# The last block of a two-stage attention and expert kernel: keys turned a tile sooner, high parts first, two operations moved

## The reference, cut to what matters

```python
qp = _phi(proj(Wq, bq)); kp = _phi(proj(Wk, bk)); v = proj(Wv, bv)   # _phi(x) = elu(x) + 1
def step(carry, inp):
    kv, ksum = carry
    kt, vt, qt = inp
    kv = kv + jnp.einsum('bhd,bhe->bhde', kt, vt)
    ksum = ksum + kt
    num = jnp.einsum('bhd,bhde->bhe', qt, kv)
    den = jnp.einsum('bhd,bhd->bh', qt, ksum)[..., None] + EPS
    return ((kv, ksum), num / den)
...
x = x + _L0_attn_ref(_layernorm(x), ...)
probs = softmax(layernorm(x) @ gate_w.T); top2_w, top2_idx = top_k(probs, 2)
counts = jnp.bincount(top2_idx.reshape(-1), length=E); keep = counts <= cap
```

## Time and profile before

| | |
|---|---|
| median of 3 runs | 1963.82 us (1962.81 to 1964.63) |
| the profiled execution | 1965.99 us |
| its span, first to last instruction | 1964.2 us |
| TensorE matmul busy | 1913.2 us (97%) |
| VectorE busy | 1588.5 us (81%) |
| ScalarE busy | 663.9 us (34%) |
| GpSimd busy | 901.9 us (46%) |
| start of block 31 on TensorE | 1921.97 us |
| last instruction of VectorE | 1961.43 us |

### The profile page before, as it was taken

The page is one execution under the profiler, slowest core; times in us unless marked ns, Lnnn a source line. Parts: engine busy times, 40 slices in busy tenths (PEclk is TensorE's granted clock), DMA queues, the critical chain, the costliest instruction groups (busy, mean ns, idle before and its releaser), DMA issues. The chain is left out here.

```text
span 1964.2 us, 60624 instructions
## 1 busy us (share of the span) xinstructions
PE 1913.2 (97%) x25420; PEld 1678.0 (85%) x25420; DVE 1588.5 (81%) x3375; ACT 663.9 (34%) x1291; POOL 901.9 (46%) x982
## 2 busy tenths in 40 slices
PE   6899999999999999999999999999999999999996
PEld 5688888888888888888888888888888888888886
DVE  5687788887788987788887988787878898878786
ACT  2333333333333333332333333333333333333331
POOL 3445345545345545345545354544345544355422
PEclk8999999999999999999999999999999999999998
DMA  5223433323333333433323333233333233343222
GB/s 182 87 82 109 130 114 120 116 80 125 125 109 125 99 102 114 124 121 114 109 90 123 120 119 120 92 110 114 125 125 109 89 107 126 113 129 121 72 73 75
DMA packets 168032, 218.02 MB, mean 111 GB/s; under 512 B 24272, under 2 KB 81616, under 8 KB 167760
## 3 DMA queue, kind: packets, MB, share of 16 engines
q1 hardware_dynamic: 165360, 213.58, 33.9%
q10 hardware_dynamic: 2400, 0.55, 0.1%
HBM read 151.02 MB, written 63.04 MB: 109 GB/s over the span
## 5 line engine op out<-in xcount | busy, mean ns | idle before, releaser
L1224 POOL TENSOR_TENSOR k_sum<-k_sum,q_raw 128x512 f32<-128x512 f32 x128 | 165.3, 1292 | 572.3 <-DVE q_raw L906 572.3
L812 ACT ACTIVATE e_tmp<-ring,bias_n 128x512 f32<-128x512 f32 x256 | 176.1, 688 | 534.0 <-PE ring L642 527.4
L895 DVE TENSOR_TENSOR s_mask<-ring,causal 128x512 f32<-128x512 f32 x512 | 314.7, 676 | 0.5 <-PE ring L707 0.5
L656 PE MATMUL ring<-wv_hi,xt_hi 128*128 128x260 f32 x1024 | 299.0, 292 | 2.4 <-DVE gate_x L927 2.4
L656 PE MATMUL ring<-wo_hi,o_hi 128*128 128x260 f32 x1024 | 288.1, 281 | 2.8 <-DVE o_lo L1144 2.6
L656 PE MATMUL ring<-wo_hi,o_lo 128*128 128x260 f32 x1024 | 290.6, 284 | 0.0
L656 PE MATMUL ring<-wv_lo,xt_hi 128*128 128x260 f32 x1024 | 288.8, 282 | 0.0
L656 PE MATMUL ring<-wv_hi,xt_lo 128*128 128x260 f32 x1024 | 288.8, 282 | 0.0
L656 PE MATMUL ring<-wo_lo,o_hi 128*128 128x260 f32 x1024 | 288.7, 282 | 0.0
L862 ACT ACTIVATE o_hi<-num_ps 128x512 fp32r<-128x512 f32 x128 | 76.6, 598 | 478.6 <-PE num_ps L735 478.4
L642 PE MATMUL ring<-xt_hi,wk_hi 128*128 128x512 f32 x512 | 210.7, 412 | 15.3 <-DVE xt_lo L971 6.9
(11 more groups left out here) (143 smaller groups left out, 4082.0 us busy)
## 6 DMA issues: line engine op xcount, KB each, us to landing
x_tok<-in_x SPq DMA_DIRECT2D x128, 256.0 KB, 3.9
res<-in_x SPq DMA_DIRECT2D x128, 256.0 KB, 2.9
out<-res SPq DMA_DIRECT2D x128, 256.0 KB, 2.0
x_in<-in_x_t SPq DMA_DIRECT2D x124, 256.0 KB, 4.4
keys_turned<-k_turned SPq DMA_DIRECT2D x112, 256.0 KB, 2.0
k_tok<-keys_turned SPq DMA_DIRECT2D x448, 64.0 KB, 2.0
x_rows<-moments_rows SPq DMA_DIRECT2D x31, 512.0 KB, 3.7
k_t<-in_wk_t SPq DMA_DIRECT2D x1, 1024.0 KB, 9.8
```

The source lines that it names most:

```text
L656: mm = pe.matmul(bank[:, 0:HW], rows[a](k), w[b][:, k, h, :], start=n == 0, stop=n == 3 * KD - 1)
L812: act.activation(e_tmp[:, m], bank, ACT.Relu, bias=bias_n[:, m, g:g + 1], scale=-1.0).then_inc(phi_relu.handle, 1)
L895: dve.tensor_tensor(s_mask[:, j], ring[:, st.bank(u)].rearrange("p (g t) -> p g t", g=KD), repeat(causal, KD), ALU.mult).then_inc(free[st. ...
L1224: pool.tensor_tensor(k_sum[:, g], k_sum[:, g], q_raw[:, g], ALU.mult).then_inc(prod.handle, 1)
```

## The change

In step 31 the keys of a tile are transposed, sent and fetched one tile sooner: those of tile 1 at the end of step 30, those of tile 2 within tile 0. In VectorE's order the transposition of (31,1) stands behind the masks of tile 3 of step 30, and that of (31,2) behind the masks of tile 0 of step 31, ahead of the residual. In SP's order the send and the fetches of (31,1) stand ahead of the store of (30,3), and those of (31,2) ahead of the store of (31,0). The output products of block 31 are sorted so that the eight with `o_hi` come first in each half; TensorE waits for `o_hi` before them and for `o_lo` before the last four. And the last two steps of part 4 stand ahead of the wait for GpSimd's power.

```diff
@@ SyncE
-                if c == 0:
+                if c == 0 and not st.alone():
                     send_keys(t, 1)
...
                     fetch_keys(t, 1)
...
-                if c == 1:
+                if c == 1 and not st.alone():
                     send_keys(t, 2)
                 if not st.has("proj") and c:
                     store(st, c - 1)
                 if not last or st.has("proj"):
                     load_res(st, *nxt)
-                if c == 1:
+                if c == 0 and st.alone():
+                    send_keys(t, 2)
+                    fetch_keys(t, 2)
+                if c == 1 and not st.alone():
                     fetch_keys(t, 2)
...
                 if last and st.has("proj"):
                     send_keys(t + 1, 0)
                     fetch_keys(t + 1, 0)
+                if last and t == n_blocks - 2:
+                    send_keys(t + 1, 1)
+                    fetch_keys(t + 1, 1)
...
                 if st.has("proj") or last:
                     store(st, c)
@@ TensorE, two_halves
-                for k in range(KD):
-                    for a, b in ((0, 0), (0, 1), (1, 0)):
-                        mm = pe.matmul(bank[:, 0:HW], rows[a](k), w[b][:, k, h, :],
-                                       start=n == 0, stop=n == 3 * KD - 1)
-                        n += 1
+                terms = [(k, a, b) for k in range(KD) for a, b in ((0, 0), (0, 1), (1, 0))]
+                if st.alone():
+                    terms.sort(key=lambda term: term[1])
+                for k, a, b in terms:
+                    if st.alone() and a == 1 and n == 2 * KD:
+                        pe.wait_ge(o_lo.handle, o_lo.at(st.lin(TPB, st.off, c + 1)))
+                    mm = pe.matmul(bank[:, 0:HW], rows[a](k), w[b][:, k, h, :],
+                                   start=n == 0, stop=n == 3 * KD - 1)
+                    n += 1
@@ TensorE, body
-                    pe.wait_ge(o_lo.handle, o_lo.at(st.lin(TPB, st.off, c + 1)))
+                    if st.alone():
+                        pe.wait_ge(o_hi.handle, o_hi.at(st.lin(TPB, st.off, c + 1)))
+                    else:
+                        pe.wait_ge(o_lo.handle, o_lo.at(st.lin(TPB, st.off, c + 1)))
@@ VectorE, last_logits
+            choose(4, range(17, CHOOSE_STEPS))
             dve.wait_ge(z_rstd.handle, 1)
             dve.tensor_tensor(z_all[:, bass.ds(tiles, TPB), :], z_b, over(rstd1, E), ALU.mult)...
-            choose(4, range(17, CHOOSE_STEPS))
@@ VectorE, body
-                if c < 2 and attn:
+                if c < 2 and attn and proj:
                     turn_keys(st.off, c + 1)
...
                 if not last and attn:
                     mask_scores(st, c + 1)
+                if c == 0 and st.alone():
+                    turn_keys(st.off, 2)
                 if last and proj:
                     mask_scores(st, 0)
+                if last and st.off == n_blocks - 2:
+                    turn_keys(st.off + 1, 1)
```

## The result

The changed kernel takes 1956.37 us (median of 6 runs, 1954.72 to 1958.11); the kernel before, run beside it, 1962.71 us (6 runs, 1961.57 to 1964.63). The ratio is 0.9966, with a 95% interval of 0.9953 to 0.9979: faster by 6.3 us by the medians. And in the first profile the parts don't add up as the sum had them: the last block, from its first state product (1916.90) to VectorE's last instruction (1952.55 us), takes 35.65 us against 39.46, which is a gain of 3.8 us, not 6.2. The other part of the shorter span lies ahead of the last block: the first store comes 6.1 us sooner, and the stretch from there to block 31 takes 1.0 us more.

What follows compares the result with a forecast made beforehand. Block 31 was taken as bound by TensorE's waits for keys and `o_lo` and a slow clock, then by VectorE. Gains of 5.9 and 0.3 us, together 6.2, off 1963.8 gave 1957.6 us, range 1956.6 to 1960.8.

Steps and rivals of the forecast that it cites:

- the sum: Block 31: 5.9 us up to the last residual half plus 0.3 in the tail, a gain of 6.2 us.
- The keys: Tiles (31,1) and (31,2): keys sent a tile sooner arrive in time, ending waits of 1.76 and 1.19 us.
- The order of the products: Block 31: eight products run before `o_lo` is needed, gaining 0.41 us in tile 0 and 0.96 in tile 3.
- The two operations in the wait: VectorE's tail: count and last product of part 4 fit into a 0.66 us wait, gaining 0.32 us.
- The chain of VectorE: Block 31: VectorE becomes the chain, `o_lo` of tile 1 at 1930.93, last residual half 5.9 us sooner.
- The choice's steps at 0.25 us each: VectorE in block 31: one more step of the choice before the next `o_lo` takes 0.25 us.
- The holes that the sum was checked by: Block 31: waits, slow clock and tail add up to 6.7 us, of which VectorE gives 0.5 back.
- The level and the range: Whole kernel: 1963.8 us before less 6.2 gives 1957.6; range 1956.6 to 1960.8.
- Late keys of (31,2): Tile (31,2): a slow send makes the keys late, 2.1 us lost, 1959.7 to 1960.7 us; chance 0.14.
- A late input of (31,2): Tile (31,2): the residual's input becomes the bound, 4.1 us lost, 1961.7; chance 0.08, with a slower kernel 0.03.
- No use of the order: Block 31: reordered products give nothing, as VectorE was the limit; 0.96 us lost, 1958.6; chance 0.06.
- A clock that falls in tile 3: Tile 3: a 0.5 us hole remains, and products at 1.2 GHz take 1.6 us more, 1959.2; chance 0.06.

Runs made afterwards that it cites:

- e17: Changed kernel, no edit, one more profiled execution: last block 34.01 us, first store at 99.3 us.
- e2: Changed kernel, no edit, timed again against the kernel before and profiled: ratio 0.9971, last block 36.00 us.
- e13: Changed kernel, no edit, one more profiled execution: last block 34.44 us, first store at 97.4 us.
- e15: Changed kernel, no edit, one more profiled execution: last block 34.20 us, first store at 98.9 us.
- bias_held: Changed kernel, with GpSimd's bias additions of tiles 1 to 3 held until VectorE has done the choice's steps of the tile before: ratio 0.9963.
- both: Changed kernel, with GpSimd's bias additions held until after the choice's steps and ScalarE's exponential of part 4 put behind `o_hi` of tile 1: ratio 0.9953.
- e11: Changed kernel, no edit, one more profiled execution: last block 35.97 us, first store at 98.9 us.
- e1: Kernel before, no edit, timed against itself and profiled: ratio 1.0006, last block 39.99 us.
- e4: Kernel before, with only the output products reordered, high parts first: ratio 0.9992, last block 40.16 us.
- e14: Kernel before, no edit, one more profiled execution: last block 42.88 us, first store at 99.4 us.
- e16: Kernel before, no edit, one more profiled execution: last block 39.75 us, first store at 101.2 us.

## Why the prediction was right and wrong

**The keys: right.** The transposition in block 30 was covered as said: the residual of (30,3) had 0.36 us of waiting left of 0.95. The sends landed after 2.79 and 2.45 us, and neither stall came back in the profiles with the keys moved, but for 0.30 us ahead of the keys of (31,2) in e17, whose block is the shortest of its kernel (34.01). The store of (31,0) went out 11.19 us after the block's begin, 11.03 by the sum, and the input behind it was never waited for.

**The order of the products: right.** In tile 3 TensorE waits 0.57 us before the low products (0.5 said), and from `o_lo` to the last half it takes 2.97 us (2.95 said).

**The two operations in the wait: right in what they give,** 0.38 us for 0.32. They no longer fit into the wait altogether, since they take 0.55, but the logits' product follows at once, 0.03 us after the power's end.

**The chain of VectorE: wrong at "so `o_lo` of tile 1 at 1930.93 instead of after a wait".** That is 8.96 us after the block's begin, and it came at 10.46 in the first profile and 9.73 where no addition was in the way (e2, e13, e15, e17). The sign that the prediction had set, `o_lo` of tiles 1 and 2 6.6 us apart without waiting for ScalarE, failed: 7.51 us apart, and 0.88 us of waiting for `o_hi`. The sum had `o_hi` at 1930.8, 0.6 us after the numerators. It left out that ScalarE has the exponential of part 4 ahead of it, which waits for the choice's second step, and this step is ready only where `o_lo` was to start. In the kernel before that step began at 1930.29 and the exponential at 1930.55, 2.5 us before `o_hi` at 1933.07, which came late because of the key wait; so it cost nothing there, and once that wait is gone it is late next. Cost 0.77 us against the sum; between `bias_held` and `both`, which differ by this alone, 0.72.

**The choice's steps at 0.25 us each: wrong where GpSimd adds.** The residual's input comes sooner and its addition falls on the choice: 0.7 us (first profile) and 1.1 (e11) on `o_lo` of tile 1, another 0.97 on that of tile 2 in both, and 0.2 to 0.6 on that of tile 3 in e13, e15 and e2. The prediction had the rule for that, and weighed it for the tail alone, where the GpSimd operation has four elements a partition. The row it was dismissed with did not bear on the 128x512 addition.

**The size of the gain: near by luck.** 6.2 us were said for the block, and the means give 5.8, but from two wrong ends that offset each other. The changed kernel's block is 35.0 on the mean instead of 33.3, for the two steps above. That of before is 40.9 instead of the 39.46 of the one execution from which the sum was taken, the shortest of seven. The holes that the sum was checked by count 1.58 us for the slow clock in tile 1. Without that fall the wait for the keys of (31,2) is 1.4 to 1.9 us longer and the block no shorter, so the term stands only together with the 1.19 behind it. What the clock does cost the block of before comes from falls in tiles 2 and 3, of which that execution had none.

**The level and the range: the step that put the time outside.** The forecast of 1957.6 us is 1963.8 − 6.2, and 1963.8 was the median of three runs of before; beside the changed kernel the same program had 1962.71 over six. Of the 1.2 us by which the time lies below the forecast, 1.1 are this level, and 0.1 the gain. The range had "half a microsecond beyond the bound for what runs differ by", and that is too little: the 11 runs of e1 reach from 1962.29 to 1967.88 us, and the medians of four sets of runs of before were 1962.71, 1963.85, 1964.54 and 1965.2. The start alone took 98.9 to 103.2 us in the seven profiles of before, so medians of six move by a microsecond or two. A low end with that much room would have held 1956.37.

**The rivals.** Late keys of (31,2): not seen, but for the 0.30 us of e17. A late input of (31,2): not seen, no residual waits for the addition in any profile. No use of the order: spoken against by the 0.94 us in tile 3 of e4, though its timed gain is not clear of nothing. A clock that falls in tile 3: seen in e2, 1.4 us (1.6 said), once in six.

## What to carry to other kernels

When a long wait goes, list what every engine has in its own queue ahead of the next signal, also on the engines that had been idle: here one exponential on ScalarE took over from a transfer. When a transfer moves, the engine operation behind it moves too, and it may land on another engine's work. And take terms that hang on the granted clock or on landings from several executions, before a single profile is treated as the kernel.

## What the runs showed of the hardware

Of VectorE and GpSimd, in the last block: a VectorE operation with both inputs in SBUF that starts while GpSimd's addition of 128x512 runs ends 0.07 to 0.09 us after that addition, whatever its own size: 0.49 to 1.31 us where 0.22 or 0.23 are usual. It is so in 18 of the 19 profiles of this study, 20 times in all; the one time that such an operation kept its 0.22 us (L1048 of e15) it had started within 0.02 us of the addition. With one input in PSUM it doesn't: in the first profile after, the residual half L1020 takes 0.42 us from 1938.46, while the addition runs from 1938.20 to 1939.48. Nor do two inputs in SBUF wait for GpSimd's power of four elements a partition: in the same profile L1111 takes 0.19 us from 1946.11 and L1113 0.19 from 1946.33, within the power's 1946.06 to 1947.08. The Trainium skill, SBUF — State Buffer, in the section on the two separate sides, has VectorE with two SBUF inputs and GpSimd take turns for whole instructions; the additions agree with it, the power does not.

The granted clock in the last block differs between executions of the same kernel: up to the last product none, one or two stretches at 0.50, which is 1.2 GHz. Ahead of the falls there were waits of TensorE: 1.76 us in the first profile of before, 3.08 and 1.90 in e14, 0.72 and 1.21 in e2. Waits also passed without a fall, of 1.90 us and of 2.63 (e16), so the length of a wait alone does not settle it. With two falls (e14) the block takes 42.88 us, with none (e16) 39.75. TensorE: Matmul & The Clock Gate of the Trainium skill describes, under HAM oscillation, how waits for transfers let the clock fall again and again; the falls behind waits for keys agree with it, but those in tile 3 (e14, e2) came behind waits for VectorE, and not every wait brought one. That a change which closes such waits also takes away the falls is likely, from one fall in six executions against six falls in seven, but not shown.
